# Scores and row maxima of two heads in two 64-row halves of the array, as fp32r high and low parts

## The reference

```python
x = x + 0.5 * ffn(layernorm(x))
x = x + attention(layernorm(x))
x = x + 0.5 * ffn(layernorm(x))

def attention(h, Wq, bq, Wk, bk, Wv, bv, Wo, bo):      # 16 heads of 16 numbers
    q, k, v = (h @ W.T + b for each, as heads)
    scores = where(causal, q @ k.T / sqrt(16), finfo.min)
    return (softmax(scores) @ v) @ Wo.T + bo
```

## Time and profile before

| | |
|---|---|
| median of 3 runs | 1269.19 us (1267.63 to 1271.1) |
| profiled execution, its own time | 1267.49 us |
| its span, first to last instruction | 1265.8 us |
| TensorE (PE) busy | 1101.6 us, 87% |
| VectorE (DVE) busy | 705.2 us, 56% |
| ScalarE (ACT) busy | 562.3 us, 44% |
| DMA, mean over the span | 29 GB/s, 37.24 MB |
| score matmuls L856 | 640, mean 356 ns |
| maxima matmuls L868 | 640, mean 361 ns |
| Exp L953 | 640, mean 541 ns |

### The profile page before, as it was taken

How to read it: one execution, slowest core, us unless ns; L and a number is a source line. 1 busy time by engine, 2 the same in 40 slices (tenths; PEclk the granted TensorE clock), 3 DMA queues, 4 the chain that set the end, 5 groups by cost and what they waited for, 6 DMA issues and landing times. The chain is left out here.

```text
span 1265.8 us, 19301 instructions
## 1 busy us (share of the span) xinstructions
PE 1101.6 (87%) x6480; PEld 718.0 (57%) x6480; DVE 705.2 (56%) x1603; ACT 562.3 (44%) x1102; POOL 110.3 (9%) x409
## 2 busy tenths in 40 slices
PE   3299999999967229888999999999966999999998
PEld 2178888888856003333333333333325888888886
DVE  7923433333367627776988888888516233333333
ACT  6422222322247016665577777776762222223222
POOL 0000000000000102332211111111121000000000
PEclk9999999999989559999999999999988999999999
DMA  5000000000027320112111101110000000000000
GB/s 172 1 1 1 1 1 1 0 0 0 0 76 178 101 58 17 49 56 66 28 47 47 41 26 32 43 47 2 1 13 1 1 1 17 1 17 0 17 0 17
DMA packets 69242, 37.24 MB, mean 29 GB/s; under 512 B 47408, under 2 KB 63024, under 8 KB 69168
## 3 DMA queue, kind: packets, MB, share of 16 engines
q1 hardware_dynamic: 69168, 36.32, 10.5%
HBM read 25.63 MB, written 10.49 MB: 29 GB/s over the span
## 5 line engine op out<-in xcount | busy, mean ns | idle before, releaser
L953 ACT ACTIVATE attn_prob<-psum 128x512 f32<-128x512 f32 (+3 forms) x640 | 297.4, 541 | 162.7 <-PE psum L856 162.0
L294 PE MATMUL psum<-ffn_xt,all_w_hi 128*128 128x512 f32 x1024 | 325.8, 399 | 4.9 <-DVE ffn_xt L375 4.9
L976 DVE TENSOR_REDUCE attn_part_max<-psum 128x1 f32<-128x512 f32 x384 | 242.2, 684 | 61.0 <-PE psum L868 59.5
L381 DVE TENSOR_TENSOR ffn_inner<-ffn_act_out,ffn_inner 128x512 fp32r<-128x512 f32 x128 | 88.6, 692 | 331.5 <-ACT ffn_inner L345 331.5
L868 PE MATMUL psum<-attn_k_st,attn_q_st 96*128 96x512 bf16 (+3 forms) x640 | 221.0, 361 | 33.8 <-DMA attn_vals<-v_rows 25.1
L856 PE MATMUL psum<-attn_q_st,attn_k_st 99*128 99x512 bf16 (+3 forms) x640 | 218.1, 356 | 32.4 <-DMA attn_q_st<-attn_max_rows 26.9
L353 ACT ACTIVATE ffn_act_out<-psum 128x512 f32<-128x512 f32 x128 | 76.5, 598 | 371.0 <-PE psum L294 370.9
L294 PEld LDWEIGHTS psum<-ffn_xt,all_w_hi 128*128 128x128 f32 x1024 | 185.3, 190 | 43.4 <-issue 5.7
L308 PE MATMUL psum<-all_w_hi,ffn_inner 128*128 128x256 f32 x1024 | 202.9, 281 | 4.1 <-DVE ffn_inner L381 4.1
L294 PE MATMUL psum<-ffn_xt,all_w_lo 128*128 128x512 f32 x512 | 203.7, 398 | 0.0
L856 PEld LDWEIGHTS psum<-attn_q_st,attn_k_st 99*128 99x128 bf16 x640 | 64.2, 102 | 208.3 <-ACT attn_prob L953 114.6
(11 more groups left out here) (96 smaller groups left out, 662.9 us busy)
## 6 DMA issues: line engine op xcount, KB each, us to landing
qk_parts<-qkv_parts SPq DMA_DIRECT2D x16, 384.0 KB, 2.6
attn_q_st<-qk_parts SPq DMA_DIRECT2D x32, 96.0 KB
attn_k_st<-qk_parts SPq DMA_DIRECT2D x16, 192.0 KB
all_x<-in_L_attn_h SPq DMA_DIRECT2D x4, 512.0 KB, 7.4
v_rows<-qkv_rows_v SPq DMA_DIRECT2D x16, 128.0 KB, 3.4
attn_q_st<-qk_parts SPq DMA_DIRECT2D x32, 64.0 KB
attn_k_st<-qk_parts SPq DMA_DIRECT2D x32, 64.0 KB
attn_k_st<-qk_parts SPq DMA_DIRECT2D x16, 128.0 KB
```

Source lines behind the costliest of these rows:

```text
L294: last = nc.tensor.matmul(psum[:, 2 * m + q % 2, :], w_part[a][:, 3 * g + m, pl, o:o + P], xt[:, k, c, pl, :], start=(n == 0), stop=(n == 5))
L381: nc.vector.tensor_tensor(inner[:, 1, u, :], act_out[:, u, :], as_f32(inner[:, 0, u, :]), ALU.subtract).then_inc(s["inner_lo"], 1)
L953: nc.scalar.activation(prob[:, n % PRING, at:BT], psum[:, S0 + n % SBANKS, at:BT], ACT.Exp).then_inc(s["exp"], 1)
L976: nc.vector.tensor_reduce(to, psum[:, bank, :], AX.X, ALU.max).then_inc(s["max_read"], 1)
```

## The change

q and k are split in two parts each, high and low, in float32r, and a score is made of three products (high-high, high-low, low-high) stacked in 3 x 16 = 48 rows. One head's stack lies on partitions 0 to 47, the other head's on 64 to 111 of the same tile; the max rows (now two) and the rows of -1 follow behind each. So a score matmul has 50 rows and a maxima matmul 48, and they use the lower or the upper 64 rows of the array. The maxima are taken in the order head 1, head 0, so that scores and maxima of different halves mostly stand side by side.

In `qkv`, ScalarE writes the high part directly (no `full`), VectorE makes the low part with one operation from PSUM, and SP writes each unit with three DMAs straight into the stacked order (`q_stack`, `k_stack`), the high part twice. Rows of -1 come from a small tile that eight DMAs write to `k_stack` at the start of the stage. In `attention`, a pair's load is four DMAs (q of each head, k with the rows of -1, v). The factor 1/4 moves into the Exp. Loads of the first two pairs stand at the start, those of pairs 2 and 3 at steps 0 and 3. GpSimd splits the maxima with two operations instead of four.

```diff
-NPART = 3
-Q_PARTS = (0, 0, 0, 1, 1, 2)
-K_PARTS = (0, 1, 2, 0, 1, 0)
+NPART = 2
-KR = len(Q_PARTS) * HD
+ROWS = 3 * HD
-LOADS = 13
+LOADS = 4
...
+                def stack_rows(dram, half, group, b):
+
+                    return dram[half * 4:half * 4 + 4, :, bass.ds(b * BT, BT)].rearrange(
+                        "r (h g d) t -> r h g d t", h=2, d=HD)[:, :, group]
...
+                        sp.wait_ge(s["minus"], 1)
+                        for hd in range(2):
+                            for b in range(NB):
+                                sp.dma_start(k_dram[:, hd * HALF + ROWS:(hd + 1) * HALF, b * BT:(b + 1) * BT],
+                                             minus[:, :]).then_inc(s["minus_out"], 16)
...
-                                sp.wait_ge(s["part_3"], b * NU + u + 1 + NU)
-                                sp.dma_start(qk_dram[NPART * kind:NPART * (kind + 1), half * P:(half + 1) * P, bass.ds(b * BT, BT)]
-                                             .rearrange("a p t -> p a t"), parts[:, u, :, :]).then_inc(s[f"part_out{u}"], 16)
+                                dram = (q_dram, k_dram)[kind]
+                                twice, once = (((0, 1), 2), ((0, 2), 1))[kind]
+                                sp.wait_ge(s["hi"], b * NU + u + 1)
+                                for group in twice:
+                                    sp.dma_start(stack_rows(dram, half, group, b), as_f32(part_hi[:, u, :])
+                                                 ).then_inc(s[f"part_out{u}"], 16)
+                                sp.wait_ge(s["lo"], b * NU + u + 1 + NU)
+                                sp.dma_start(stack_rows(dram, half, once, b), as_f32(part_lo[:, u, :])
+                                             ).then_inc(s[f"part_out{u}"], 16)
...
-                                act.wait_ge(s["part_3"], b * NU + u + 1)
-
-                                nc.scalar.activation(full[:, u, :], psum[:, u, :], ACT.Identity,
-                                                     scale=SCALE if kind == 0 else 1.0,
-                                                     bias=bias_q[:, half:half + 1] if kind == 0 else bias[:, 1, half:half + 1]
-                                                     ).then_inc(s["full"], 1)
-                                part(b, u, 0)
+                                act.wait_ge(s[f"part_out{u}"], (b + 1) * 48)
+                                nc.scalar.activation(part_hi[:, u, :], psum[:, u, :], ACT.Identity,
+                                                     bias=bias[:, kind, half:half + 1]).then_inc(s["hi"], 1)
...
-                                lesser(b, u, 0)
+                                kind, half = divmod(u, 2)
+                                dve.wait_ge(s["hi"], b * NU + u + 1)
+                                nc.vector.scalar_tensor_tensor(part_lo[:, u, :], psum[:, u, :], bias[:, kind, half:half + 1],
+                                                               as_f32(part_hi[:, u, :]), ALU.add, ALU.subtract).then_inc(s["lo"], 1)
...
-                return begin[2 * before[n] + 2] + 1 if before[n] >= 0 else -1
+                return begin[2 * before[n] + 2] + 1 if before[n] >= 0 else (-1, -1, 0, 3)[n]
...
-                mine = [(e, hd) for e, a in enumerate(chunk_at) if a == d for hd in range(2)]
+                mine = [(e, hd) for e, a in enumerate(chunk_at) if a == d for hd in (1, 0)]
...
-                q_st = tb("q_st", [P, 2, QSLOTS, 2 * BT], BF16)
-                k_st = tb("k_st", [P, 2, KSLOTS, BT], BF16)
+                q_st = tb("q_st", [P, QSLOTS, 2 * BT], F32R)
+                k_st = tb("k_st", [P, KSLOTS, BT], F32R)
...
+                def head(hd, rows=ROWS):
+                    return slice(hd * HALF, hd * HALF + rows)
...
-                            nc.tensor.matmul(psum[:, S0 + n % SBANKS, at:BT], k_st[rows, hd, k0 + c, o * P:(o + 1) * P],
-                                             q_st[rows, hd, b, g % 2 * BT + at:g % 2 * BT + BT], start=True, stop=True).then_inc(s["scored"], 1)
+                            nc.tensor.matmul(psum[:, S0 + n % SBANKS, at:BT], k_st[rows, k0 + c, o * P:(o + 1) * P],
+                                             q_st[rows, b, g % 2 * BT + at:g % 2 * BT + BT], start=True, stop=True).then_inc(s["scored"], 1)
...
-                            nc.tensor.matmul(psum[:, M0 + n % MBANKS, 0:cols], q_st[0:KR, hd, b, g % 2 * BT + i * P:g % 2 * BT + (i + 1) * P],
-                                             k_st[0:KR, hd, k0 + c, 0:cols], start=True, stop=True).then_inc(s["max_scored"], 1)
+                            nc.tensor.matmul(psum[:, M0 + n % MBANKS, 0:cols], q_st[head(hd), b, g % 2 * BT + i * P:g % 2 * BT + (i + 1) * P],
+                                             k_st[head(hd), k0 + c, 0:cols], start=True, stop=True).then_inc(s["max_scored"], 1)
...
-                        nc.vector.memset(k_st[KR:P, :, :, :], -1.0).then_inc(s["ones"], 1)
```

More of the change, by code:

```diff
@@ L778, in _ @@
                                 max_row(g)
-                            for n in range(QSLOTS, NL):
+                            for n in range(2, NL):
                                 for j in range(LOADS):
                                     if free_at(n) + j // 3 == d:
-                                        if j == 0:
+                                        if j == 0 and before[n] >= 0:
                                             sp.wait_ge(s["weighted"], begin[2 * before[n] + 2])
@@ L904, in gather @@
                             last.then_inc(s["x_full"], 1)
-                        pe.wait_ge(s["ones"], 1)
                         for e, a in enumerate(chunk_at):
                             if a < 0:
-                                for hd in range(2):
+                                for hd in (1, 0):
                                     maxima(e, hd)
                             if e == ends[0] + 3:
-                                pe.wait_ge(s["made"], 14)
+                                pe.wait_ge(s["made"], 13)
                                 turn_max(0)
@@ L953, in _ @@
                                 nc.scalar.activation(prob[:, n % PRING, at:BT], psum[:, S0 + n % SBANKS, at:BT],
-                                                     ACT.Exp).then_inc(s["exp"], 1)
+                                                     ACT.Exp, scale=HD ** -0.5).then_inc(s["exp"], 1)
                             for t in turned(d):
@@ L981, in maxima @@
                                                                op0=ALU.add, op1=ALU.max, accum_out=to).then_inc(s["max_read"], 1)
-                            if e == ends[g] and hd == 1:
+                            if e == ends[g] and hd == 0:
                                 dve.wait_ge(s["max_read"], n + 1)
```

118 lines of the change are left out of this document (40 added, 78 removed).

## The result

| | before | after |
|---|---|---|
| median | 1268.6 us | 1343.5 us |
| runs | 1267.6 to 1271.1 | 1331.5 to 1346.1 |
| ratio | | 1.057 (1.053 to 1.061) |
| profiled execution, its span | 1267.5, 1265.8 | 1346.0, 1344.3 |
| mean PEclk | 0.957 | 0.876 |

What follows compares the result with a forecast made beforehand. TensorE was taken to set the pace, with VectorE 15% behind in the second half. From 1267.5 us, head -28, first half -14, second half -20 and qkv +7 gave 1212.5, on the median 1214 us; range 1192 to 1256.

Steps and rivals of the forecast that it cites:

- The head, -28: Start of attention: fewer loads ahead of the maxima bring the first score at 21.5 instead of 49.4 us; -28 us.
- `qkv`, +7, upper bound +24: Blocks of qkv: more bytes written make each block 1.4 us longer, plus a longer queue at the end; +7 us.
- q and k writes run at 341 GB/s: In qkv: rate of q and k writes alone, 181 / 0.53, so 3.15 MB take 9.2 us a block.
- Rival 1: In qkv: doubled writes decide, v's queue behind them while VectorE waits; upper bound +24, about 1233 us; chance 0.10.
- The second half, -20: Attention's second half: paired matmuls shorten a pair of heads from 38.96 to about 36 us; -20 us in all.
- chain of 2.46 plus 0.09: Second-half step: Exp chain of 2.46 us plus 0.09 for the longer weight load makes 2.55 us against 2.74.
- gain nothing: End of attention: the last 12 steps have no maxima and so get no gain.
- The first half, -14: Attention's first half: a pair of heads takes 16.3 us for 18.19, over 7.5 pairs; -14 us.
- rival 4: Attention loop: less busy TensorE, half its rows used, gets 1.2 GHz; +160, about 1405 us; 0.05 with others above 1290.
- with 121 of 137 us busy the clock was 0.95: First half before the change: argument against a falling clock, the low part being the cold start.
- half of its rows in use: Attention loop: part of the reason given why TensorE could be granted only 1.2 GHz.
- Rival 3: Attention's matmuls: row halves stream in turn or weight loads lie open; 1278 or 1257 us; chance 0.15.

Runs made afterwards that it cites:

- e2: The kernel before with only the order of attention's loads changed (two pairs ahead, third and fourth from steps 0 and 3); 1253.2 us, ratio 0.987.
- e1: The changed kernel with stack rows interleaved, so qkv's writes have 128 as outermost size and matmuls use 64 rows; 1270.8 us over four runs.
- e5: The changed kernel with both parts, stacks and maxima's rows in bfloat16 instead of float32r; 1258.9 us, ratio 0.992.
- e8: e5 with e1's interleaved layout: 64 rows a matmul instead of 48 and 50, and the faster writes; 1205.5 us, ratio 0.949.
- e10: e8 with every score and maxima matmul over all 128 rows, zeros in the other head's half of q, nothing in pairs; 1221.0 us, ratio 0.961.
- e6: e5 with both heads' stacks in rows 0 to 63, so matmuls of 48 or 50 rows run one after the other; 1591.7 us, ratio 1.255.
- e7: e1 (float32r) with every score and maxima matmul over all 128 rows, nothing in pairs, and three q slots for four; 1302.6 us, ratio 1.025.
- e3: The changed kernel with each maxima matmul issued twice; 1361 and 1417 us in two runs.
- e11: The changed kernel with its slow writes, only the scores' matmuls using 64 rows of a half instead of 50; 1321.0 us, ratio 1.038.
- e9: e1 run once more, unchanged; 1262.6 us over six runs, ratio 0.993.
- e12: e10 with halves in pairs for the groups of the second half, except the last group; 1209.7 us, ratio 0.954.

## Why the prediction was wrong

The direction was wrong and the time 129 us off: 1214 forecast, 1343.5 measured, outside 1192 to 1256.

- **The head, -28**: right, -28.8, and by the path foreseen: maxima at 8.2 us, first score when VectorE was through its chunks. e2 shows 23.3 of it on its own, with 26 loads ahead, of which its first half gives 9.1 back.
- **`qkv`, +7, upper bound +24**: failed, +31.5. The step that failed was "q and k writes run at 341 GB/s", taken from writes whose target has 128 rows as its outermost dimension, while the new ones have 8 x 16. The diff shows that pattern. They ran at 182. The prediction took the engines' busy share as free to rise from 0.53 to 1; with the new pattern it stayed at 0.56 to 0.63. e1, which changes the pattern of these writes, takes 30.8 of the 31.5 back. Rival 1 had the right place and mechanism (v's writes behind the others, VectorE waiting for v's landing), but its worst rate, 256 GB/s, was itself taken from the old pattern.
- **The second half, -20**: the step "chain of 2.46 plus 0.09" was mis-sized. Pairs do stream together, 0.23 us each, and the chain does decide; but with fp32r it is 2.74, not 2.55: 0.10 more in front of the Exp, 0.18 more between the fourth score and `weigh`. e5 shows 2.53 with bfloat16 in its place. At full clock the pair came to 39.27 and not 36, which is +2.2 over seven pairs. The rest of the +20.5 is the clock before 695.5 (about +3) and the last pair of heads, +15.4: in e1, whose clock held 1.00 there, that pair took 35.5 us (copies 895.28 and 930.75), so 13.0 of it are the clock and 2.4 the float32r steps, where the prediction had "gain nothing".
- **The first half, -14**: failed, +53.9, by rival 4, "the clock falls", to which I gave 0.05. At full clock a pair took 17.56 in the changed kernel itself (copies 594.82 and 612.38) and 17.57 in e1, against 16.3 forecast and 18.19 before, so -14 was mis-sized too, by an estimate about -5. The pairs that repeat steadily there took over 17.5 in every run, and with bfloat16 the halves gain nothing (e8 17.85, e10 17.62); what holds a pair at 17.6 was not taken apart. The failure is the sentence that set rival 4 aside: "with 121 of 137 us busy the clock was 0.95". That row is of matmuls with 96 and 99 rows. Nor was its low part all cold start: between 590 and 600 the clock was 0.83, behind 10 us in which TensorE was busy for 6.1. e6 against e10 shows that busy time says little: 0.50 at 120 of 120 us with 48 and 50 rows, 1.00 at 90 of 100 with 128. Rival 4's own words had the cause in them, "half of its rows in use". Its price, 160 us for both halves, was too high: in the second half the clock came back, and stayed until the last pair of heads.
- **Rival 3** (halves do not cover each other) fell: starts are equal. The Trainium skill's rule of weight loads (TensorE: Matmul & The Clock Gate, "Part 3: Packing small matmuls"), that a load overlaps matmuls in flight only when its row group differs, is not borne out here: every second matmul follows one of its own half, and they still start 0.23 us apart (835.60, 835.83). Loads are open only at the first score, behind `weigh`, and at the fourth, behind its wait for the Exp.

Of the 77 us against the kernel before, then, the writes are +31.5, the clock about +75 (59 in the first half, 3 at the start of the second, 13 in the last pair of heads), float32r steps in the second half +5, the matmuls of the first half at full clock about -5, and the head -28.8.

Shown is that more rows lift the clock; not settled is what else does: why the changed kernel's clock rose at 593, fell at 624, and held from 695.5 to 979, when its matmuls have the same rows all along; why it falls in e7 with all 128 rows; and why in e1, e3, e8 and e11 it falls in one execution more than in the next (1254 to 1282, 1361 to 1417, 1201 to 1221, 1316 to 1343). Even the kernel before had one execution of 1463.3 us with a mean clock of 0.746. What separates the two halves of the program in that respect (the length of runs between `gather`s, the 512-column share) wasn't tried.

## What to carry to other kernels

Before two small matmuls are put side by side, ask what few rows do to the clock: matmuls on 50 of 128 rows can lower it for everything around them, and rows of zeros up to the half's 64 cost nothing (36.10 us a pair of heads with 48 and 50 rows in e5 and with 64 in e8). Read a DMA's rate only from transfers with the same outermost dimension on both sides; a rearrangement of rows so that the 128 partitions stay outermost was worth 31 us here. And when a change does several things, price each at the clock and the data type that it will have, since here one part, the order of the loads, gained 15 us alone.

## What the runs showed of the hardware that was not expected

- The granted clock followed the rows in use: 0.50 with 48 and 50 rows alone on the array (e6), 0.50 to 0.65 with pairs of them (changed kernel, e5), 0.79 with scores of 64 (e11), 0.88 to 0.91 with pairs of 64 (e1, e8), 0.86 with 128 in float32r (e7), 1.00 with 128 in bfloat16 (e10), all between 480 and 580 us. Taken from the first score to the 16th copy instead, the order is nearly the same: e6 0.50, the changed kernel 0.58, e5 0.59, e11 0.75, e9 0.76, e1 0.81, e8 0.83, e7 0.90, e10 1.00. The Trainium skill (TensorE: Matmul & The Clock Gate, "Part 1: The HAM clock gate") has the clock follow how busy TensorE is; by that e6, busy in all of its 120 us, should have been at full clock.
- Two matmuls of row halves started within 10 ns of each other and took 0.23 us for both, 512 columns each; a half and a full height in turn took 0.64 for both (e12).
- float32r cost 3.2 to 3.4 us a pair of heads (14 steps) over bfloat16 for equal columns, with weight loads of 0.18 us for 0.10.
- Writes with 8 x 16 x 512 as target ran at 182 GB/s, the same bytes with 128 x 512 at 314.
